# Two attentions and a feed-forward in one kernel: the next batch's values and both sets of transposes take other places in TensorE's row

## The chip, the cores and the metric

The kernel runs on one core of one Trainium2 chip. The metric is the device time of one execution in microseconds (us). The time before is the median of three runs, 399.38 us (396.07 to 399.92).

## The reference, cut to what matters

```python
# x, ctx: (16, 128, 128); 16 heads of 64
def self_attention(x):                    # over the 128 positions of a batch
    Q, K, V = x @ W_Q + b_Q, x @ W_K + b_K, x @ W_V + b_V
    P = softmax(Q @ K.T / 8)
    return (P @ V) @ W_O + b_O

def cross_attention(x1, ctx):             # per position, over the HEADS, not the positions
    q, k, v = x1 @ Wq.T + bq, ctx @ Wk.T + bk, ctx @ Wv.T + bv
    P2 = softmax(einsum('bshd,bsgd->bshg', q, k) / 8)
    out = einsum('bshg,bsgd->bshd', P2, v)          # then transposed and reshaped
    return out @ Wo.T + bo

x1 = layernorm(x  + self_attention(x))
x2 = layernorm(x1 + cross_attention(x1, ctx))
x3 = layernorm(x2 + feed_forward(x2))     # rms norm, up, gelu, down
```

## The kernel before, in words

The 16 batches go through a pipeline that is written out by hand as 16 calls of `step(s, ...)` on each engine (steps 3 to 14 are a loop of three rounds of four), followed by a tail that is written out instruction by instruction. Nothing is scheduled by a tool: each engine runs its own list in order, and semaphores with counts join the lists. In step s TensorE (PE) works on three batches at once. Part a is the scores and softmax of batch s, part bc the self-attention output and the cross-attention scores of batch s-1, part d the cross-attention output of batch s-2. Each group of four batches shares the projections of queries and keys, so a step also has a phase, s modulo 4: in phase 3, 0 and 1 there is group work (blocks A to D of `project_qk`, then E and F of `project_k2`) in the row, in phase 2 none.

PE's row in one step before the change, by the helpers' names:

- `transpose_p(s-1, 1)`: the second half of the transposes of the softmax result P of batch s-1, 8 heads, to PSUM banks 1 and 6. It waits for `p_ready`, which GpSimd (POOL) gives after `over_sum`. ScalarE (ACT) copies each bank to `pt` (`transposed`).
- blocks of `project_qk` or `project_k2`, in phases 0 and 1.
- `values(phase)`: the values of batch s, six products, to banks 7 and 0. They are 128x128 by 128x512 products of operands split in a high and a low part. ACT copies them out (`values_out`).
- `weighted(s)`: P transposed times the values, batch s-1. VectorE (DVE) copies the two halves out (`attention_out`, semaphore `ot_ready`).
- `scores(0)`: half of the scores of batch s, to banks 7 and 0. DVE takes their maxima (`score_max`), ACT the exponentials.
- `project_o`: the output projection of the self-attention, batch s-1. It waits for `ot_ready`, both halves.
- `transpose_p2`, then `scores(1)`, then `values2(0)` and `values2(1)` (the context's values, banks 2 and 3, copied out by DVE's `values2_out`, semaphore `v2s_ready`).
- the transpose of x1 (bank 7) and `transpose_x2` (bank 0), which ACT copies out.
- `weighted_v2`, `project_q2` (banks 2 and 3), `transpose_p(s, 0)` (the first half for batch s), in phase 3 block A, `project_o2` (the second output projection), `scores2`, and in phases 3 and 0 the first two units of the next block.

After `scores2` DVE runs `pick_own` (four operations) and `max2`. POOL then subtracts the maximum (`minus_max2`), ACT takes the exponential (`exp2`) and DVE the sums (`sums2`). In phases 2 and 3 DVE's list has this order at the start of a step:

```python
for u in range(2):
    attention_out(s, u)
    if d and not projecting:
        (sums2, inverse_sums2)[u](s)
```

So `sums2` stands between the two `attention_out` there. In phases 0 and 1 it stands earlier, beside the group work.

DVE's list goes on with `score_max(0)`, `score_max(1)`, `x2_out`, `stats1`, `block_diagonal` twice, `x1_out`, `inverse_sums(0)`, `score_max(2)`, `values2_out(0)`, `score_max(3)`, `values2_out(1)`, `regrouped`, `q2_out` twice, in phase 0 `c_low`, `inverse_sums(1)`, `stats2`, `pick_own`, `max2`. SyncE (SP) issues 16 DMAs per step, which spread the context values for `weighted_v2`.

Of the kernel before, what the change touches and what calls it, by code (L numbers as in the profile page):

```python
# [50 lines left out]
def build(nc, x_nat, x_t, ctx_t, w_qk, w_v, w_o, b_qk, b_v, b_o,  # L51
# [10 lines left out]
    with ctx:  # L62
# [110 lines left out]
        X1T, X2T = 7, 0  # L173
# [298 lines left out]
        def _(act):  # L472
# [75 lines left out]
            def step(s, h, g, phase, a, bc, d):  # L548
                par, b_par = phase % 2, 1 - phase % 2

                def transposed(u):

                    act.wait_ge(mm_t, 4 * s + u + 1 if u < 2 else 4 * s - 4 + u + 1)
                    dst, src = pt_part(u)
                    nc.scalar.activation(dst, src, ACT.Copy).then_inc(pt_ready, 1)  # L555
# [10 lines left out]
                def values_out(s, par):  # L566
                    for u in range(2):
                        act.wait_ge(mm_v, 2 * s + u + 1)
                        nc.scalar.activation(v[par][:, u * BANK:(u + 1) * BANK], bank(V_BANK[u]), ACT.Copy).then_inc(v_ready, 1)
# [13 lines left out]
                if bc:  # L583
                    transposed(2)
                    transposed(3)
# [15 lines left out]
                if a and bc:  # L601
                    values_out(s, par)
# [10 lines left out]
                if not static or s > 2:  # L613
                    x2_transposed(s - 1, X2T)
                if a:
                    exponentials(2)
# [4 lines left out]
                if phase == 3 and not static:  # L621

                    act.wait_ge(mm_v, 2 * s + 2)
                    x_high(g + 1)
# [9 lines left out]
                if static and s == 0:  # L634
# [3 lines left out]
                    split_hi(8)  # L638
                if a:
# [7 lines left out]
            for u in (2, 3):  # L647
                act.wait_ge(mm_t, 4 * (B - 1) + u + 1)
                dst, src = pt_part(u)
                nc.scalar.activation(dst, src, ACT.Copy).then_inc(pt_ready, 1)  # L650
# [33 lines left out]
        def _(dve):  # L684
# [140 lines left out]
            def step(s, h, g, phase, a, bc, d):  # L825
# [62 lines left out]
                if static and s == 0:  # L888
# [14 lines left out]
                    return  # L903
                if a and not (static and s == 1):
# [9 lines left out]
                if phase == 3 and not static:  # L914
                    x_low(g + 1)
# [132 lines left out]
        def _(pe):  # L1048
# [135 lines left out]
            def values(phase):  # L1184
                own = slice(phase * T, (phase + 1) * T)
                for u in range(2):
                    cols = slice(u * BANK, (u + 1) * BANK)
                    nc.tensor.matmul(bank(V_BANK[u]), xg_lo[:, own], wv_hi[:, cols], start=True, stop=False)  # L1188
# [25 lines left out]
            def step(s, h, g, phase, a, bc, d):  # L1214
# [64 lines left out]
                if bc:  # L1279
                    transpose_p(s - 1, 1)  # L1280
# [13 lines left out]
                if a and bc:  # L1294

                    pe.wait_ge(pt_ready, 4 * s - 4 + 2)
                    values(phase)
# [7 lines left out]
                elif a:  # L1305
# [4 lines left out]
                    pe.wait_ge(v_ready, 2 * s + 2)  # L1310
# [18 lines left out]
                if bc:  # L1329
# [3 lines left out]
                    for u in range(2):  # L1333
# [3 lines left out]
                        values2(u, own)  # L1337
                    if static and s == 1:
                        pe.wait_ge(in_perm, 16)
                    if a:  # L1340

                        pe.wait_ge(exp_ready, 4 * s + 1)
                    pe.wait_ge(x1_ready, s)
                    nc.tensor.transpose(bank(X1T, T), x1[:], perm[:]).then_inc(mm_x1t, 1)
                    if late:
                        if a:

                            pe.wait_ge(exp_ready, 4 * s + 2)
# [13 lines left out]
                if bc:  # L1362
                    project_q2(s, 1)
                if static and s == 0:
# [7 lines left out]
                    values(0)  # L1372
                    project_k2(0, "F", lambda r: read_k2(r, "E"), units=(0, 1))
                    pe.wait_ge(in_ident, 16)

                    pe.wait_ge(v_ready, 2)
                if a:
                    if late:

                        pe.wait_ge(xnt_ready, s - 2)  # L1380
                    transpose_p(s, 0)
                if static and s == 0:

                    project_k2(0, "F", lambda r: read_k2(r, "E"), units=(2, 3))
# [6 lines left out]
                if d:  # L1391
# [3 lines left out]
                    project_o2(s)  # L1395
                if phase == 3 and not static:
# [21 lines left out]
            transpose_p(B - 1, 1)  # L1418
# [149 lines left out]
```

## Time and profile before

| | us |
|---|---|
| median of 3 runs | 399.38 |
| lowest, highest | 396.07, 399.92 |
| the profiled execution, whole | 397.88 |
| its span, first to last instruction | 396.1 |
| PE busy in the span | 386.1 |
| DVE busy | 285.3 |
| ACT busy | 239.7 |
| POOL busy | 147.7 |

The span is the part of the profiled execution that the trace covers. 1.8 us lie around it. An engine's busy time is the union of its instructions' times. One minus its share is the time that it stood waiting.

### The profile page before, as it was taken

What the parts mean: (1) busy time and instruction counts of PE and PEld (TensorE: products, weight loads), DVE (VectorE), ACT (ScalarE), POOL (GpSimd) and SP (SyncE); (2) the same over time, 40 slices, a digit from 0 to 9 for tenths busy, and PEclk for the clock granted to TensorE, in tenths of its full rate; (3) what the DMA queues carried; (4) which work ended last, traced back from release to release, by engine and by line L of the source; (5) the groups of instructions that cost most, each with busy time, mean ns of one, the idle gap of its engine ahead of it and who ended that gap; (6) DMA issues with size and microseconds to landing.
All of it is one profiled execution on the core that took longest, in us unless ns stands there. A gap on an engine that the chain in (4) does not pass through costs nothing.

```text
span 396.1 us, 16460 instructions
## 1 busy us (share of the span) xinstructions
PE 386.1 (97%) x6836; PEld 335.3 (85%) x6836; DVE 285.3 (72%) x660; ACT 239.7 (61%) x815; POOL 147.7 (37%) x224
## 2 busy tenths in 40 slices
PE   8999899999999999999999999999999999999995
PEld 8787788878888888878988888878988888888985
DVE  4677778776749688776848778667757878677555
ACT  5685585745567475745668466655667566556451
POOL 0642445421414454422414454323315455323214
PEclk9999999999999999999999999999999999999999
DMA  7910212310100213110101113100101111211001
GB/s 238 370 48 8 47 31 44 88 31 7 38 22 15 51 29 96 33 25 8 42 16 25 40 35 89 40 18 8 38 20 30 40 36 25 48 40 25 28 29 53
DMA packets 43760, 19.37 MB, mean 49 GB/s; under 512 B 36592, under 2 KB 41200, under 8 KB 43696
## 3 DMA queue, kind: packets, MB, share of 16 engines
q1 hardware_dynamic: 42880, 16.88, 16.5%
q0 software_dynamic: 528, 1.45, 1.0%
q8 instruction: 54, 0.88, 0.9%
q10 hardware_dynamic: 288, 0.07, 0.1%
q14 instruction: 10, 0.08, 0.1%
HBM read 8.95 MB, written 1.05 MB: 25 GB/s over the span
## 4 chain that ended last, share of the span: by engine, by line
PE 91%; SPq 3%; DVE 2%; issue 1%; ACT 1%; DMA 1%; POOL 1%; POOLq 0%; DVEq 0%
PE ps L1255 8%; PE ps L1200 8%; PE ps L1077 7%; PE ps L1168 7%; PE ps L1105 7%; PE ps L1180 7%; PE ps L1057 5%; PE ps L1157 5%; PE ps L1059 5%; PE ps L1058 5%; PE ps L1096 4%; PE ps L1210 4%; PE ps L1133 3%; SPq L323 3%; PE ps L1188 3%; PE ps L1194 2%
## 5 line engine op out<-in xcount | busy, mean ns | idle before, releaser
L562 ACT ACTIVATE p<-ps,neg_max 128x128 f32<-128x128 f32 x256 | 90.0, 382 | 38.9 <-DVE neg_max L832 38.7
L409 POOL TENSOR_TENSOR p<-p,row_inv 128x1024 f32<-128x1024 f32 x32 | 60.7, 1897 | 64.4 <-DVE row_inv L838 64.4
L555 ACT ACTIVATE pt<-ps 128x512 f32<-128x512 f32 x62 | 34.3, 619 | 47.1 <-PE ps L1157 46.9
L562 ACT ACTIVATION_READ_ACCUMULATOR p<-ps,neg_max 128x1 f32 x256 | 57.4, 224 | 0.0
L832 DVE TENSOR_REDUCE neg_max<-ps 128x4 f32<-128x512 f32 x64 | 41.7, 675 | 5.1 <-PE ps L1255 4.0
L778 DVE TENSOR_TENSOR ot<-ps,bv 128x512 f32<-128x512 f32 x32 | 22.0, 689 | 25.0 <-PE ps L1180 24.8
L1168 PE MATMUL ps<-x1t,wq 128*64 128x64 f32 x1024 | 34.4, 224 | 2.1 <-issue 1.7
L1255 PE MATMUL ps<-kt,qt 64*64 64x128 f32 x1024 | 35.2, 275 | 0.0
L1168 PEld LDWEIGHTS ps<-x1t,wq 128*64 128x64 f32 x1024 | 31.8, 138 | 3.8 <-issue 2.7
L1105 PE MATMUL ps<-wo,ot 128*128 128x128 f32 x256 | 32.3, 279 | 0.5 <-DVE qt L810 0.5
L1200 PE MATMUL ps<-wo,ot 128*128 128x128 f32 x256 | 32.7, 281 | 0.0
L1180 PEld LDWEIGHTS ps<-pt,v 128*64 128x64 f32 x512 | 27.6, 137 | 5.8 <-ACT pt L555 3.3
L1255 PEld LDWEIGHTS ps<-kt,qt 64*64 64x64 f32 x1024 | 27.6, 132 | 5.4 <-issue 5.3
L1200 PEld LDWEIGHTS ps<-wo,ot 128*128 128x128 f32 x256 | 29.9, 191 | 2.7 <-issue 2.6
L1180 PE MATMUL ps<-pt,v 128*64 128x128 f32 x512 | 31.5, 276 | 0.0
L1105 PEld LDWEIGHTS ps<-wo,ot 128*128 128x128 f32 x256 | 30.0, 192 | 1.7 <-DVE qt L810 0.6
L1077 PE MATMUL ps<-cg,wk 128*64 128x128 f32 x512 | 29.9, 274 | 0.0
L402 POOL TENSOR_TENSOR rn<-ssm,minus_half 128x1 f32<-128x1 f32 x16 | 8.8, 549 | 56.3 <-DVE ssm L769 56.3
L1077 PEld LDWEIGHTS ps<-cg,wk 128*64 128x64 f32 x512 | 27.8, 137 | 1.0 <-issue 0.5
L1057 PE MATMUL ps<-xg_hi,wqk_hi 128*128 128x512 f32 x62 | 25.4, 409 | 0.4 <-issue 0.4
L1058 PE MATMUL ps<-xg_lo,wqk_hi 128*128 128x512 f32 x62 | 24.5, 395 | 0.0
L1059 PE MATMUL ps<-xg_hi,wqk_lo 128*128 128x512 f32 x62 | 24.5, 395 | 0.0
(158 smaller groups left out, 827.6 us busy)
## 6 DMA issues: line engine op xcount, KB each, us to landing
v<-v2s SPq DMA_DIRECT2D x256, 32.0 KB
xg<-x_t SPq DMA_DIRECT2D x4, 256.0 KB, 2.6
cg<-ctx_t SPq DMA_DIRECT2D x4, 256.0 KB, 2.7
wo<-w_o SPq DMA_DIRECT2D x2, 512.0 KB, 9.3
xres<-x_nat SPq DMA_DIRECT2D x15, 64.0 KB, 1.8
pt<-w_qk SPq DMA_DIRECT2D x3, 256.0 KB, 4.1
out<-x2b SPq DMA_DIRECT2D x3, 256.0 KB, 2.3
x2b<-w_v SPq DMA_DIRECT2D x1, 512.0 KB, 6.4
```

The source lines that it names most:

```text
L409: nc.gpsimd.tensor_tensor(ph, ph, row_inv[:, 8 * half:8 * half + 8].unsqueeze(2).to_broadcast([T, 8, T]), ALU.mult).then_inc(p_ready, 1)
L562: last = nc.scalar.activation(p[:, hd * T:(hd + 1) * T], bank(S_BANK[q])[:, pos * T:(pos + 1) * T], ACT.Exp, bias=neg_max[:, hd:hd + 1], a ...
L832: nc.vector.reduce_max(neg_max[:, first:first + 7:2], bank(S_BANK[q]).rearrange("p (h k) -> p h k", h=4), AX.X, negate=True).then_inc(max_ ...
L1057: nc.tensor.matmul(out_cols, w_hi_cols, m_hi, start=True, stop=False)
L1058: nc.tensor.matmul(out_cols, w_hi_cols, m_lo, start=False, stop=False)
L1059: return nc.tensor.matmul(out_cols, w_lo_cols, m_hi, start=False, stop=True)
L1077: last = nc.tensor.matmul(bank(BLOCK_BANKS[blk][r])[64 * ih:64 * ih + 64, i * 128:(i + 1) * 128], wk2[:, hd * DH:(hd + 1) * DH], own, star ...
L1105: last = nc.tensor.matmul(bank(O2, D), ot2[:, k * 128:(k + 1) * 128], wo2[:, k * D:(k + 1) * D], start=k == 0, stop=k == K - 1)
L1168: last = nc.tensor.matmul(bank(Q2[u])[64 * ih:64 * ih + 64, i * HALF:(i + 1) * HALF], wq2[:, hd * DH:(hd + 1) * DH], x1t[:, ih * HALF:(ih ...
L1180: last = nc.tensor.matmul(bank(PV_BANK[u])[64 * (i % 2):64 * (i % 2) + 64, (i // 2) * T:(i // 2 + 1) * T], v[b_par][:, hd * DH:(hd + 1) * ...
L1200: last = nc.tensor.matmul(bank(O, D), ot[:, c * T:(c + 1) * T], wo[:, c * D:(c + 1) * D], start=c == 0, stop=c == NC - 1)
L1255: mm = nc.tensor.matmul(bank(S_BANK[2 * half + i % 2])[qh * HALF:(qh + 1) * HALF, (i // 2) * T:(i // 2 + 1) * T], qt[rows, first:first + H ...
```

## The change

`values` leaves its place ahead of `weighted`. It now computes the values of the next batch, s+1, right behind `values2`, and waits for the exponentials that read banks 7 and 0. The x1 and x2 transposes stand behind it. They go to banks 2 and 3 instead of 7 and 0, and so wait until DVE has copied the context values out of these banks (`v2s_ready`). Both halves of the transposes of P of batch s stand together behind `project_o2` (in phase 3 the first half stays ahead of block A), ahead of `scores2`. None is left at the start of a step. ACT's list follows: `exponentials(2)`, then the two copies of the next values, then the copy of x1 transposed, and all four copies of P transposed at the end of a step. DVE's list changes in one place: in phase 3 `x_low` (the low part of the next group's x) stands ahead of `score_max(2)`, since the next values need it in this step.

```diff
-        X1T, X2T = 7, 0
+        X1T, X2T = 2, 3
...
 # ScalarE
-                if bc:
-                    transposed(2)
-                    transposed(3)
...
-                if a and bc:
-                    values_out(s, par)
...
-                if bc:
+                if phase == 3 and not static:
+
+                    act.wait_ge(mm_v, 2 * s + 2)
+                    x_high(g + 1)
+                if bc:
+                    exponentials(2)
+                    if not (static and s == B - 1):
+                        values_out(s + 1, b_par)
                     act.wait_ge(mm_x1t, s)
                     nc.scalar.activation(x1t[:], bank(X1T, T), ACT.Copy).then_inc(x1t_ready, 1)
...
                 if a:
                     transposed(0)
                     transposed(1)
                 if phase == 3 and not static:
                     qk_out(g + 1, "A")
+                if a:
+                    transposed(2)
+                    transposed(3)
...
 # VectorE
+                if phase == 3 and not static:
+                    x_low(g + 1)
                 if a and not (static and s == 1):
                     score_max(2)
...
 # TensorE
-                if bc:
-                    transpose_p(s - 1, 1)
...
-                if a and bc:
-
-                    pe.wait_ge(pt_ready, 4 * s - 4 + 2)
-                    values(phase)
                 if bc:
                     weighted(s, b_par)
...
-                    pe.wait_ge(v_ready, 2 * s + 2)
                     scores(0)
...
                         values2(u, own)
+                    if s < B - 1:
+                        if phase == 3:
+                            pe.wait_ge(x_lo, g + 2)
+
+                        values((phase + 1) % GB, lambda u: pe.wait_ge(exp_ready, 4 * s + u + 1))
...
-                    if a:
-
-                        pe.wait_ge(exp_ready, 4 * s + 1)
+
+                    pe.wait_ge(v2s_ready, 2 * s - 1)
                     pe.wait_ge(x1_ready, s)
                     nc.tensor.transpose(bank(X1T, T), x1[:], perm[:]).then_inc(mm_x1t, 1)
                     if late:
-                        if a:
-
-                            pe.wait_ge(exp_ready, 4 * s + 2)
+
+                        pe.wait_ge(v2s_ready, 2 * s)
                         transpose_x2(s - 1, X2T)
...
                     project_o2(s)
+                if a:
+                    if phase < 3 or static:
+
+                        if s < B - 1:
+                            pe.wait_ge(v_ready, 2 * s + 4)
+                        transpose_p(s, 0)
+                    transpose_p(s, 1)
```

The first place is PE's row from the second output projection of a step of phase 1 to the output projection of the next step, of phase 2. `L1105` is `project_o2`, `L1157` `transpose_p`, `L1210` `scores2`, `L1188` to `L1190` `values`, `L1180` `weighted`, `L1255` `scores`, `L1200` `project_o`. Before:

```order
L1157 MATMUL ps<-ident,p 128x64 [waits p_ready,xnt_ready]
L1105 MATMUL ps<-wo,ot 128x128 [waits ot2_by_dve,ot2_by_act,q2_ready]
L1210 MATMUL ps<-kb,qt 64x64 [waits k2_by_act,k2_by_dve,q2_ready]
L1157 MATMUL ps<-ident,p 128x64 [waits p_ready]
L1188 MATMUL ps<-wv_hi,xg_lo 128x512 [waits pt_ready]
...
L1180 MATMUL ps<-pt,v 64x128 [waits v_ready,pt_ready]
...
L1255 MATMUL ps<-kt,qt 64x128 [waits v_ready]
...
L1200 MATMUL ps<-wo,ot 128x128 [waits ot_ready,s2_ready]
```

After, in the changed kernel's line numbers (each two or three lower):

```order
L1102 MATMUL ps<-wo,ot 128x128 [waits ot2_by_dve,ot2_by_act,q2_ready]
...
L1154 MATMUL ps<-ident,p 128x64 [waits p_ready,v_ready]
...
L1154 MATMUL ps<-ident,p 128x64 [waits p_ready]
...
L1208 MATMUL ps<-kb,qt 64x64 [waits k2_by_act,k2_by_dve,q2_ready]
...
L1177 MATMUL ps<-pt,v 64x128 [waits v_ready,pt_ready]
...
L1253 MATMUL ps<-kt,qt 64x128 x16
L1198 MATMUL ps<-wo,ot 128x128 [waits ot_ready,s2_ready]
```

Between `scores2` and `project_o` stand only `weighted` and `scores(0)` now. The second half of the transposes and `values` have left this stretch.

The second place is PE's row from the context's values to `weighted_v2` (`L1096`) in a late step. `L1194` to `L1196` are `values2`, `L1344` is the transpose of x1, `L1112` that of x2. Before:

```order
L1194 MATMUL ps<-wv_hi,cg_lo 128x512 [waits c_lo,k2_by_dve]
...
L1196 MATMUL ps<-wv_lo,cg_hi 128x512
L1344 MATMUL ps<-perm,x 128x128 [waits x1_ready,exp_ready]
L1112 MATMUL ps<-ident,xn 128x128 [waits xn_ready,exp_ready]
L1096 MATMUL ps<-pt,v 64x64 [waits pb_ready,sum1_ready,v2_moved]
```

After:

```order
L1192 MATMUL ps<-wv_hi,cg_lo 128x512 [waits c_lo,k2_by_dve]
...
L1194 MATMUL ps<-wv_lo,cg_hi 128x512
L1186 MATMUL ps<-wv_hi,xg_lo 128x512 [waits exp_ready]
...
L1186 MATMUL ps<-wv_hi,xg_lo 128x512 [waits exp_ready]
...
L1339 MATMUL ps<-perm,x 128x128 [waits x1_ready,v2s_ready]
L1109 MATMUL ps<-ident,xn 128x128 [waits xn_ready,v2s_ready]
L1093 MATMUL ps<-pt,v 64x64 [waits pb_ready,sum1_ready,v2_moved]
```

The six products of the next values (`L1186` to `L1188`) have come in, and the two transposes wait for `v2s_ready` in place of `exp_ready`.

## Rows read from the trace of the kernel before

**Rows 1.** The page, part 1: busy time, share of the span, instructions.

```profile
PE 386.1 (97%) x6836; PEld 335.3 (85%) x6836; DVE 285.3 (72%) x660; ACT 239.7 (61%) x815; POOL 147.7 (37%) x224
```

**Rows 2.** The page, part 4: the chain that ended last, shares by engine.

```profile
PE 91%; SPq 3%; DVE 2%; issue 1%; ACT 1%; DMA 1%; POOL 1%; POOLq 0%; DVEq 0%
```

**Rows 3.** Windows: stretch, its length, busy us of each engine, clock, DMA.

```profile
31.00:47.00 16.00, 14.59 (x302) 12.45 (x300) 11.12 (x24) 9.68 (x40) 5.72 (x7) 1.00 0.12 26
117.00:134.00 17.00, 17.00 (x370) 14.74 (x366) 13.16 (x31) 10.48 (x43) 6.62 (x9) 1.00 0.11 27
```

**Rows 4.** Timeline of PE, step 9 (phase 1) into step 10: start, us, line.

```profile
206.94 2.05 PE L1200 MATMUL ps<-wo,ot 128*128 128x128 f32 x16
...
211.67 0.27 PE L1344 MATMUL ps<-perm,x 128*128 128x128 f32 x1
...
215.96 0.71 PE L1157 MATMUL ps<-ident,p 64*128 64x64 f32 x16
216.60 2.05 PE L1105 MATMUL ps<-wo,ot 128*128 128x128 f32 x16
...
219.67 0.71 PE L1157 MATMUL ps<-ident,p 64*128 64x64 f32 x16
221.89 1.97 PE L1180 MATMUL ps<-pt,v 128*64 128x128 f32 x32
...
224.82 2.05 PE L1200 MATMUL ps<-wo,ot 128*128 128x128 f32 x16
```

**Rows 5.** Timeline of DVE, the same stretch.

```profile
211.40 0.64 DVE L832 TENSOR_REDUCE neg_max<-ps 128x4 f32<-128x512 f32 x1
...
213.15 0.68 DVE L788 TENSOR_TENSOR v2s<-ps,bv_row 128x512 f32<-128x512 f32 x1
...
216.06 0.69 DVE L810 TENSOR_TENSOR qt<-ps,bq 128x512 f32<-128x512 f32 x1 [0.69 <-PE ps L1168]
216.67 0.19 DVE L838 RECIPROCAL row_inv<-row_sum 128x8 f32<-128x8 f32 x1
...
219.81 0.48 DVE L818 TENSOR_SCALAR s<-ps,own_j 128x256 f32<-128x256 f32 x1 [0.22 <-PE ps L1210]
...
221.88 0.42 DVE L728 TENSOR_REDUCE mx<-s 128x16 f32<-128x256 f32 x1
...
223.64 0.41 DVE L732 TENSOR_REDUCE sum<-s 128x16 f32<-128x256 f32 x1
223.97 0.68 DVE L778 TENSOR_TENSOR ot<-ps,bv 128x512 f32<-128x512 f32 x1
```

**Rows 6.** Timeline of POOL, the same stretch.

```profile
216.94 1.90 POOL L409 TENSOR_TENSOR p<-p,row_inv 128x1024 f32<-128x1024 f32 x1 [3.07 <-DVE row_inv L838]
...
222.38 0.62 POOL L373 TENSOR_TENSOR s<-s,mx 128x256 f32<-128x256 f32 x1 [1.90 <-DVE mx L728]
```

**Rows 7.** Timeline of ACT, the same stretch.

```profile
203.69 1.16 ACT L569 ACTIVATE v<-ps 128x512 f32<-128x512 f32 x2
...
210.52 0.44 ACT L523 ACTIVATE xn<-x,rn 128x128 f32<-128x128 f32 x1
...
212.36 0.37 ACT L562 ACTIVATE p<-ps,neg_max 128x128 f32<-128x128 f32 x1
...
213.74 1.13 ACT L519 ACTIVATE ot<-ps 128x512 f32<-128x512 f32 x1
...
223.04 0.42 ACT L514 ACTIVATE s<-s 128x256 f32<-128x256 f32 x1 [0.44 <-POOL s L373]
```

**Rows 8.** Timeline of ACT and of DVE, step 11 (phase 3).

```profile
248.97 0.65 ACT L484 ACTIVATE xg_hi<-xg 128x512 fp32r<-128x512 f32 x1
...
249.65 0.69 DVE L695 TENSOR_TENSOR xg_lo<-xg,xg_hi 128x512 fp32r<-128x512 f32 x1 [0.56 <-ACT xg_hi L484]
```

**Rows 9.** The chain in order of time: start, us, line; two products of `values`.

```profile
202.49 0.43 PE ps L1188
...
203.39 0.23 PE ps L1188
```

More of the change, by code:

```diff
@@ L551, in transposed @@
                 def transposed(u):
[L553 removed]
+                    act.wait_ge(mm_t, 4 * s + u + 1)
                     dst, src = pt_part(u)
@@ L609, in step @@
                     normed_x2(s - 1)
+                if phase == 3 and not static:
+                    act.wait_ge(mm_v, 2 * s + 2)
+                    x_high(g + 1)
                 if bc:
+                    exponentials(2)
+                    if not (static and s == B - 1):
+                        values_out(s + 1, b_par)
                     act.wait_ge(mm_x1t, s)
                     nc.scalar.activation(x1t[:], bank(X1T, T), ACT.Copy).then_inc(x1t_ready, 1)
-                if not static or s > 2:
+                elif a:
+                    exponentials(2)
+                if s_late(s):
                     x2_transposed(s - 1, X2T)
-                if a:
-                    exponentials(2)
                 if phase == 0 and bc and a:
@@ L620, in step @@
                     c_high(g)
-                if phase == 3 and not static:
-                    act.wait_ge(mm_v, 2 * s + 2)
-                    x_high(g + 1)
                 if static and s == B - 1:
@@ L638, in step @@
                     split_hi(8)
+                    values_out(1, 1)
                 if a:
@@ L643, in step @@
                     qk_out(g + 1, "A")
+                if a:
+                    transposed(2)
+                    transposed(3)
             run_steps(act, step)
[L647 to L650, printed above, removed]
             exp2(B)
@@ L913, in step @@
                     values2_out(s, 1, d)
-                if phase == 3 and not static:
-                    x_low(g + 1)
                 if static and s == B - 1:
@@ L1182, in weighted, with values @@
                     last.then_inc(mm_pv, 1)
-            def values(phase):
+            def values(phase, before):
                 own = slice(phase * T, (phase + 1) * T)
@@ L1187, in values @@
                     cols = slice(u * BANK, (u + 1) * BANK)
+                    before(u)
                     nc.tensor.matmul(bank(V_BANK[u]), xg_lo[:, own], wv_hi[:, cols], start=True, stop=False)
@@ L1362, in step @@
                 if bc:
+                    if late:
+                        pe.wait_ge(xnt_ready, s - 2)
                     project_q2(s, 1)
@@ L1371, in step @@
                     pe.wait_ge(w_lo, WV_SPLIT)
-                    values(0)
-                    project_k2(0, "F", lambda r: read_k2(r, "E"), units=(0, 1))
+                    values(0, lambda u: None)
+                    project_k2(0, "F", lambda r: read_k2(r, "E"))
+                    values(1, lambda u: pe.wait_ge(v_ready, u + 1))
                     pe.wait_ge(in_ident, 16)
[L1376 to L1380, printed above, removed]
+                if phase == 3 and not static:
+                    pe.wait_ge(v_ready, 2 * s + 4)
                     transpose_p(s, 0)
-                if static and s == 0:
-                    project_k2(0, "F", lambda r: read_k2(r, "E"), units=(2, 3))
                 if phase == 3 and not static:
@@ L1416, in _ @@
                 step(s, s // 2, s // GB, s % GB, s < B, 1 <= s <= B, s >= 2)
-            transpose_p(B - 1, 1)
             pe.wait_ge(wup_split, 2)
```

6 lines of the change are left out of this document (3 added, 3 removed).

## Prediction

> **What bounds the kernel now.** I read the page's busy times first, then the chain that ended last, then windows over single steps, then the timelines of one step engine by engine. PE is busy for 386.1 of 396.1 us [rows 1], and the chain is PE for 91% [rows 2]. A window of one step shows no idle time on PE at all, 17.00 of 17.00 us, with the granted clock at 1.00 [rows 3]. The change removes no product: the same matmuls run in another order. So there are at most the 10 us that PE idles to be gained. The question is the other one: PE has no waits now because each result that it needs is ready just before. Where the new order asks for one earlier, the difference appears in full. So I laid the new order of each engine over the rows of one step, with the rows' durations, and looked for the operand that comes last.
>
> I count from M, the start of `project_o` (206.94 in step 9), and from E, the end of `scores2` (219.67, where the next row starts) [rows 4]. Durations below are distances between starts, since neighbouring instructions overlap.
>
> **First term: project_o waits for DVE, steps of phases 2 and 3.** After E came `transpose_p` and `values`, 221.89-219.67 = 2.22 us, then `weighted` and `scores(0)`, 224.82-221.89 = 2.93 us [rows 4]. Now only the 2.93 us lie between E and `project_o`. What DVE must do in this time has not moved. `pick_own` starts 0.14 after E and `max2` at 2.21 [rows 5]. It runs 0.33 to the next start, so DVE is free at E+2.54. The first `attention_out` takes 0.61 to the next start, as `q2_out` of the same size does (216.06 to 216.67) [rows 5]. Behind it stands `sums2`, which needs the exponential. POOL's subtraction starts at E+2.71 and takes 0.62, and ACT's exponential 0.42 from E+3.37 to E+3.79 [rows 6, 7]. ACT is free by then: its four copies end near E+0.4. `sums2` runs from E+3.83 for 0.33 (223.64 to 223.97), the second `attention_out` from E+4.16 for 0.68, and `project_o` can start at E+4.89. The wait is 4.89-2.93 = 1.96 us. It hits the entries of steps 2, 3, 6, 7, 10, 11, 14 and 15. The first of them is counted with the start below, so 7 x 1.96 = 13.7 us. In phases 0 and 1 ten units of `project_qk` (each half of `values`, some 0.75 us) or six of `project_k2` (each half of `weighted`, 0.95 us) lie between E and `weighted` and still cover DVE's part.
>
> **Second term: the x2 transpose waits for values2_out.** From M on DVE works without a gap, and it ends `values2_out(1)` at 213.15+0.68 = M+6.89, released at M+6.93 or so; PE can go at M+6.97 [rows 5]. PE comes to the x1 transpose at M+4.73 now [rows 4]. With six products of 0.233 us in front (1.40) this is M+6.13, and the x2 transpose would start at M+6.24. It waits 0.73 us. The exponentials that `values` itself waits for end at 210.52 = M+3.58 [rows 7], before PE asks, and cost nothing. In steps 4, 5, 6, 8, 9, 10, 12, 13, 14 that is 9 x 0.73 = 6.6 us. Behind it ACT's new order would bite next: `score_max(2)` ends at M+5.10, four exponentials take 213.74-212.36 = 1.38, two copies of values 1.16, the copy of x1 0.28, so x1 transposed is ready at M+8.0, and PE asks for it behind `weighted_v2`, which has as many products as `scores2` (1.09 us), at M+8.17. That is a margin of 0.2 us, so I put it at nothing; had it no cover it would be worth its lateness in each step. Step 2, without an x2 transpose, waits for it by 0.5.
>
> In phase 3 `x_low` stands ahead of `score_max(2)`. `x_high` takes 0.65 us on ACT [rows 8] and can start at M+4.01, after the copy at 210.52 (0.44 long) [rows 7]. `x_low` runs from M+4.72 and takes 0.60 of DVE's time. DVE would have been at `score_max(2)` at M+4.46 [rows 5], so all behind it comes 0.86 later, and the x2 transpose at M+7.8 instead of 6.24: 1.56 us, 3 x 1.56 = 4.7 us. Step 15 has no next values in front. Its x2 transpose comes up at M+4.84 and waits until M+6.97: 2.1 us, of which 0.85 us replace waits that this step has already. I take 1.3.
>
> **Third term: the second half of the transposes waits for POOL.** `q2_out(1)`, the reciprocal and `over_sum` are a chain: from the end of `project_q2` (215.96 in the rows) to the end of `over_sum` at 216.94+1.90 = 218.84 [rows 4 to 6] plus its release it is 2.94 us. PE needs this half after `project_o2` (216.60 to 219.67 is 3.07 us and holds it and `scores2`; as many products as `project_o`, 2.05 less an overlap of 0.07, it takes 1.98, which leaves 1.09 for `scores2`) and the first half (215.96 to 216.60, 0.64), 2.62 us later: a wait of 0.32 us in steps 2, 5, 6, 9, 10, 13, 14, 15, 2.6 us. In phase 0 `c_low`, of the size of `x_low`, stands before the reciprocal, 0.61 more: 0.93 x 3 = 2.8 us. In phase 3 block A covers it.
>
> **Fourth term: the moved half was a cover.** Units 2 of blocks B and E wait for `pick_own`, which is through at E+2.1. Before, two units and a set of transposes (0.64) stood between. Now only the units: six products like `values` for block B (2.22-0.64 = 1.58), a wait of 0.5, and 32 like `weighted` for block E (1.97 less the overlap), 0.2. Three of each make 2.1 us.
>
> **Start.** In step 0 both halves stand together ahead of `weighted`: it waits until ACT has made three copies after the first half, 3 x 0.55, against 0.64 of PE work, 1.05 us. The first half waits for the last copy of `values`, some 0.65. I take 1.7 us. Step 1 to 2 has the 1.96 of the first term and a third term over 1 us, but it idles already: PE is busy 14.59 of 16 us from 31 to 47 [rows 3], and these 1.4 us are swallowed. I take 1.9 us.
>
> **What the order gives back.** The first product of this kind behind another kind takes 0.43 instead of 0.23 us on the chain [rows 9]. `values` behind `values2` pays that no more in 11 batches, and block B, no longer split, in 3: 14 x 0.2 = 2.8 us gained.
>
> **What is neutral.** SP's 16 DMAs now wait for `weighted_v2` (M+8.2) instead of `values2_out` (M+6.9). They have a whole, longer step to land before the next `weighted_v2`, so nothing. The tail has the same rows in the same order but for the moved half, whose 0.64 us a wait for x1 takes up. Banks 7 and 0 are free when `scores(0)` comes.
>
> **The sum.** 13.7 + 6.6 + 0.5 + 4.7 + 1.3 + 2.6 + 2.8 + 2.1 + 1.7 + 1.9 - 2.8 = 35.1 us. The profiled execution took 397.9 us, its span 396.1. So 433.0 us. That execution is 1.5 us under the median of 399.4. Steps stay whole: each term is counted from an M or an E on which both engines meet, so they add and do not overlap. I forecast 433.
>
> A rule is weighed here. The rows show a granted clock of 1.00 in both windows, also in the one with 1.4 us of idle PE [rows 3]. The Trainium skill, "TensorE: Matmul & The Clock Gate", section "A second HAM failure mode: psum-queue depth-cycling", says that a PE which idles briefly between groups of matmuls, again and again, can drop back to the low clock. By the rows the new waits of up to 2 us cost only themselves and the sum is 433; by the rule it would be the third rival below. The trace of before speaks for the rows, though its waits are shorter and rarer.
>
> **Rivals.** *The waits are hidden (the other side).* If DVE delivered `attention_out(1)` within 2.93 us of E and `values2_out(1)` by M+6.2, only the gain of 2.8 us would stay: 395.1 us. The mechanism is the cheaper change between kinds of product [rows 9], at `values2` to `values`, and it decides once the waits are under 0.1 us a step, 15 steps. Against it: DVE needs 2.40 + 0.60 + 0.68 = 3.7 us from E by its own work alone, without POOL and ACT. Chance 0.03.
>
> *Half the first term.* If `sums2` finds its operand earlier than I chain it, the second `attention_out` ends at E+2.54+0.60+0.33+0.68 = 4.15 at best, and the wait is 1.25 instead of 1.96 us; with the second term absorbed by half as well, 7 x 0.7 + 3.3 + 2.4 = 10.6 less: 422 us. For it speaks that sub-chains of three engines are long in my sum, against it that POOL's and ACT's starts are read, not assumed. Chance 0.14.
>
> *The clock falls.* No row has the low level of 1.2 GHz. At half the clock a stretch takes twice as long, an estimate. If `project_o`, which stands right behind each of the 8 long waits, ran so, that is 8 x 2.05 = 16 us more: 449 us. Chance 0.05.
>
> *ACT's copies bite.* If the margin of 0.2 us at x1 transposed is not there, ACT adds 0.3 to 0.5 us in 13 steps, 4 to 6 us: 438 us. Chance 0.14. The forecast itself has 0.64.
>
> **How the numbers follow.** The range from 421 to 441 takes in the forecast with some 4 us either way for the rounding of fifteen small waits, the half term and the copies, and leaves out 0.08. The runs of before spread over 1%, about what a measurement of this kernel can tell from no change. Only the first rival is not slower by over 1%: it gives 0.7% faster, so same 0.03, and I keep 0.01 for faster by more. Slower by over 1%: 0.96.
>
> **What the profile after would show.** PE's busy share falls from 97% to near 90%, with about 2 us idle before `project_o` in steps of phases 2 and 3, released by DVE's `ot`, and about 0.7 us before the x2 transpose, released by DVE's `v2s`, 1.5 in phase 3. `transpose_p` shows short waits for POOL's `p`. The chain has less PE and more DVE, POOL and ACT. Each round of four steps is about 9 us longer. If `project_o` does not wait, the first term is wrong and with it the forecast. If PE's clock is under 1.00 in a window, the third rival holds. If the copy of x1 transposed releases `project_q2`, ACT's order is what I undervalued.

## The result

The changed kernel takes 438.0 us (median of four runs, 436.28 to 439.31) against 398.2 us before, a ratio of 1.101 with a 95% interval of 1.097 to 1.105. The forecast was 433, with a range of 421 to 441. The profiled execution took 439.3 us, its span is 437.5.

The page of the changed kernel, parts 1 and 4: busy times and the chain that ended last, shares by engine.

```profile
PE 396.1 (91%) x6836; PEld 343.3 (78%) x6836; DVE 287.7 (66%) x660; ACT 240.9 (55%) x815; POOL 149.2 (34%) x224
...
PE 65%; DVE 20%; issue 6%; POOL 5%; ACT 2%; SPq 1%; DVEq 0%; POOLq 0%; DMA 0%
```

The same 6836 matmuls keep PE busy for 10.0 us more than before [rows 1], and PE idles 437.5 - 396.1 = 41.4 us instead of 10.0. The chain was PE for 91% [rows 2]; now DVE, POOL and ACT hold 27% of it. The span itself is longer by 41.4 us too (396.1 before, the same figure by chance). Of these, 31.4 us are new idle time of PE and 10.0 us are longer busy time. Most of the 10.0 goes with the clock, of which more below: in the first experiment, whose profiled execution has no fall of the clock, PE is busy for 388.4 us. The waits by what PE waited for (us in total, times, longest):

```profile
PE ps L1198 <- DVE ot L775: 16.2, 8, 2.3
PE ps L1109 <- DVE v2s L785: 6.7, 11, 0.9
PE ps L1154 <- POOL p L409: 5.7, 11, 1.4
PE ps L1054 <- DVE s L819: 1.7, 3, 0.6
...
PE ps L1177 <- ACT pt L554: 1.1, 1, 1.1
...
PE ps L1339 <- DVE v2s L785: 0.8, 1, 0.8
PE ps L1074 <- DVE s L819: 0.8, 3, 0.3
```

These are the prediction's terms one by one: `project_o` (L1198) on `attention_out`, the x2 transpose (L1109) on `values2_out`, the second half of the transposes (L1154) on `over_sum`, blocks B and E (L1054, L1074) on `pick_own`. The 1.1 us of `weighted` (L1177) belong to the start. The timeline of PE for step 9 into step 10, the stretch of [rows 4], shows them in place:

```profile
231.42 2.05 PE L1198 MATMUL ps<-wo,ot 128*128 128x128 f32 x16
...
238.37 0.33 PE L1109 MATMUL ps<-ident,xn 128*128 128x128 f32 x1 [0.58 <-DVE v2s L785]
...
244.68 0.71 PE L1154 MATMUL ps<-ident,p 64*128 64x64 f32 x16 [0.26 <-POOL p L409]
...
246.42 1.97 PE L1177 MATMUL ps<-pt,v 128*64 128x128 f32 x32
248.31 1.10 PE L1253 MATMUL ps<-kt,qt 64*64 64x128 f32 x32
251.40 2.81 PE L1198 MATMUL ps<-wo,ot 128*128 128x128 f32 x16 [1.98 <-DVE ot L775]
254.00 0.63 PE L1081 MATMUL ps<-ident,p 128*128 128x128 f32 x2
254.57 1.70 PE L1253 MATMUL ps<-kt,qt 64*64 64x128 f32 x32
```

M is 231.42, E is 246.42 and the next M 251.40. The x2 transpose starts at M+6.95 (forecast M+6.97), the next `project_o` at E+4.98 (forecast 4.89). The chain in order of time shows the path across the three other engines from E on:

```profile
248.63 0.43 DVE mx L725
249.06 0.07 issue
249.13 0.63 POOL s L373
...
249.79 0.42 ACT s L514
...
250.24 0.42 DVE sum L729
250.66 0.61 DVE ot L775
251.26 0.14 issue
251.40 0.68 PE ps L1198 x4
```

DVE's `attention_out` of the second half (250.66) starts only when `sums2` (250.24) is through, which has waited for POOL and ACT.

What I gave a chance of its own stands in the last three rows of the timeline: `project_o` takes 2.81 us behind the wait instead of 2.05, and `scores(1)` 1.70 instead of 1.10. Windows over this place (stretch, length, busy us by engine, granted clock, DMA):

```profile
231.42:246.42 15.00, 14.17 (x309) 12.37 (x305) 9.90 (x24) 10.34 (x42) 6.63 (x9) 1.00 0.12 26
246.42:251.40 4.98, 3.00 (x70) 2.61 (x65) 4.12 (x10) 0.52 (x2) 0.62 (x1) 1.00 0.22 46
251.40:255.40 4.00, 4.00 (x34) 3.67 (x38) 2.88 (x11) 3.19 (x17) 2.18 (x5) 0.63 0.03 6
```

Behind the 1.98 us in which PE stood, the granted clock has a mean of 0.63 in four us. Windows of 1 us over the whole span show five such falls, in steps 1, 6, 7, 10 and 11, each with 1 us windows at 0.50, the low level of 1.2 GHz. The kernel before had none in its profiled execution. Four of the falls stand behind the wait of `project_o`. The fall of step 1 stands behind two other waits, 0.73 and 1.13 us, and `weighted`, which takes 1.97 us in the kernel before, takes 3.35 there:

```profile
33.60 3.35 PE L1177 MATMUL ps<-pt,v 128*64 128x128 f32 x32 [1.13 <-ACT pt L554]
```

### The profile page after: what moved, and what is told of

Read it like the earlier page. It is cut to its first block, busy times and chain, and to the rows that moved or that the text cites. A ratio compares the mean times of both kernels' runs of the same rounds, so it can differ in the third digit from the quotient of the medians.

```text
span 437.5 us, 16468 instructions
## 1 busy us (share of the span) xinstructions
PE 396.1 (91%) x6836; PEld 343.3 (78%) x6836; DVE 287.7 (66%) x660; ACT 240.9 (55%) x815; POOL 149.2 (34%) x224
## 4 chain that ended last, share of the span: by engine, by line
PE 65%; DVE 20%; issue 6%; POOL 5%; ACT 2%; SPq 1%; DVEq 0%; POOLq 0%; DMA 0%
PE ps L1198 8%; PE ps L1165 7%; PE ps L1074 5%; PE ps L1253 5%; PE ps L1054 4%; PE ps L1055 4%; PE ps L1056 4%; PE ps L1102 4%; PE ps L1093 4%; DVE s L819 4%; POOL p L409 3%; DVE v2s L785 3%; PE ps L1177 3%; PE ps L1208 3%; DVE neg_max L829 3%
## 5 line engine op out<-in xcount | busy, mean ns | idle before, releaser
L561 ACT ACTIVATION_READ_ACCUMULATOR p<-ps,neg_max 128x1 f32 x256 | 55.2, 216 | 0.0
L1198 PE MATMUL ps<-wo,ot 128*128 128x128 f32 x256 | 36.4, 301 | 16.2 <-DVE ot L775 16.2
L1198 PEld LDWEIGHTS ps<-wo,ot 128*128 128x128 f32 x256 | 33.2, 209 | 19.4 <-issue 19.4
L1253 PE MATMUL ps<-kt,qt 64*64 64x128 f32 x1024 | 37.1, 286 | 0.0
L1253 PEld LDWEIGHTS ps<-kt,qt 64*64 64x64 f32 x1024 | 29.4, 140 | 6.3 <-issue 6.1
L1165 PEld LDWEIGHTS ps<-x1t,wq 128*64 128x64 f32 x1024 | 31.4, 138 | 3.1 <-issue 1.7
L1177 PE MATMUL ps<-pt,v 128*64 128x128 f32 x512 | 32.7, 283 | 1.1 <-ACT pt L554 1.1
L1102 PE MATMUL ps<-wo,ot 128*128 128x128 f32 x256 | 32.3, 279 | 0.0
L807 DVE TENSOR_TENSOR qt<-ps,bq 128x512 f32<-128x512 f32 x32 | 22.1, 692 | 14.6 <-PE ps L1165 14.5
L1177 PEld LDWEIGHTS ps<-pt,v 128*64 128x64 f32 x512 | 29.0, 141 | 3.3 <-issue 1.5
L1102 PEld LDWEIGHTS ps<-wo,ot 128*128 128x128 f32 x256 | 30.0, 192 | 1.2 <-DVE qt L807 0.2
L1074 PE MATMUL ps<-cg,wk 128*64 128x128 f32 x512 | 29.7, 274 | 0.8 <-DVE s L819 0.8
L373 POOL TENSOR_TENSOR s<-s,mx 128x256 f32<-128x256 f32 x16 | 10.1, 633 | 59.3 <-DVE mx L725 59.3
L1074 PEld LDWEIGHTS ps<-cg,wk 128*64 128x64 f32 x512 | 27.8, 137 | 2.3 <-DVE s L819 1.5
L1154 PE MATMUL ps<-ident,p 64*128 64x64 f32 x512 | 22.6, 228 | 6.6 <-POOL p L409 5.7
L721 DVE COPY ot<-ps 128x512 f32<-128x512 f32 x16 | 18.0, 1125 | 15.3 <-PE ps L1093 15.3
```

The costliest lines, as they stand in the source:

```text
L561: last = nc.scalar.activation(p[:, hd * T:(hd + 1) * T], bank(S_BANK[q])[:, pos * T:(pos + 1) * T], ACT.Exp, bias=neg_max[:, hd:hd + 1], a ...
L807: nc.vector.tensor_tensor(qt2[:].rearrange("p (t h) -> p t h", h=H)[:, :, heads], bank(Q2[u]).rearrange("p (h t) -> p t h", h=8), bq2[:, h ...
L1074: last = nc.tensor.matmul(bank(BLOCK_BANKS[blk][r])[64 * ih:64 * ih + 64, i * 128:(i + 1) * 128], wk2[:, hd * DH:(hd + 1) * DH], own, star ...
L1102: last = nc.tensor.matmul(bank(O2, D), ot2[:, k * 128:(k + 1) * 128], wo2[:, k * D:(k + 1) * D], start=k == 0, stop=k == K - 1)
L1154: mm = nc.tensor.transpose(bank(T_BANK[2 * half + e])[:, i * HALF:(i + 1) * HALF], p[rows, hd * T:(hd + 1) * T], ident[rows, rows])
L1165: last = nc.tensor.matmul(bank(Q2[u])[64 * ih:64 * ih + 64, i * HALF:(i + 1) * HALF], wq2[:, hd * DH:(hd + 1) * DH], x1t[:, ih * HALF:(ih ...
```

## The experiments

The kernels were run in three sets, each next to the kernel before, which had medians of 397.3 to 397.8 us there. Clocks below are those of the profiled execution unless others are named.

**The first term: what project_o waits for.** One edit in DVE's list of the changed kernel:

```diff
                     for u in range(2):
                         attention_out(s, u)
-                        if d and not projecting:
-                            (sums2, inverse_sums2)[u](s)
+                    if d and not projecting:
+                        sums2(s)
+                        inverse_sums2(s)
```

> The changed kernel with one edit in VectorE's list: in phases 2 and 3 sums2 and inverse_sums2 stand behind both attention_out instead of between them. Theory (project_o waits for the second attention_out, which waits for sums2 and so for POOL and ACT): the wait of 1.96 us falls to about 0.9, 7 or 8 times 1.1 = 8.6 us less, and the granted clock no longer falls behind the waits of steps 6, 7, 10 and 11, some 5 us more: 424 us. Rival (any wait there drops the clock, however short): 429 us. Rival (the wait is for pick_own alone, sums2 is beside the point): 438 us, unchanged.

Measured: 430.2 us, ratio to the kernel before 1.083 (1.078 to 1.088). PE's timeline in this run, from step 6 to the start of step 7:

```profile
148.66 2.02 PE L1199 MATMUL ps<-wo,ot 128*128 128x128 f32 x16 [0.98 <-DVE ot L775]
155.90 0.33 PE L1110 MATMUL ps<-ident,xn 128*128 128x128 f32 x1 [0.86 <-DVE v2s L785]
...
168.17 2.02 PE L1199 MATMUL ps<-wo,ot 128*128 128x128 f32 x16 [1.22 <-DVE ot L775]
```

The wait falls from 1.98 to 0.98 us in the first of these steps and to 1.22 in the second, and no 1 us window of the profiled execution is under 1.00 in clock. So the serial path over POOL and ACT was about half of the wait. The rival that `pick_own` alone was to blame falls. The rival that any wait drops the clock had the nearer number, 429 us, but not the mechanism: the waits of `project_o` of 0.98 to 1.93 us did not drop it here. The other three executions have mean clocks of 0.991 to 0.996, so a fall or two in them is likely (the run below with one fall has 0.996).

The size was 6 us short of what I expected, and the second row says why: the x2 transpose now starts at 155.90-148.66 = M+7.24 instead of M+6.95. DVE's sums did not vanish, they stand behind M now, where DVE bounds PE again. In phase 3 they delay `x_low`: the next values wait 2.1 us for it in three steps by PE's list, against 0.9 us in the run filled with 8 products below, and the step from 168.17 to 199.27 takes 31.10 us, where the filled run takes 30.46.

**The clock.** Products of a zero tile fill the wait, in the changed kernel. They go into the bank which `project_o` then overwrites, so the output stays the same:

```diff
                     ring_wait(2)
+                    if phase >= 2:
+                        for _ in range(12):
+                            nc.tensor.matmul(bank(O, D), warm[:], warm[:], start=True, stop=True)
                     pe.wait_ge(ot_ready, 2 * s)
```

> The changed kernel with 12 additional 128x128x128 products of the zero tile warm ahead of project_o in phases 2 and 3, into project_o's bank, which project_o then overwrites: about 1.5 us of extra PE work inside the wait of 1.96 us, so that PE stands idle for 0.5 us only. Theory (part of the loss is the clock, which falls behind the long wait): the wait for VectorE ends at the same point, the clock stays at 1.00 in steps 6, 7, 10 and 11, and the time falls by 4 falls of up to 1.7 us, less what the slower products hide in the next wait: 432 to 434 us. Rival (the fallen clock costs nothing, since PE waits anyway): 438 us.

Measured: 440.6 us, ratio 1.108 (1.104 to 1.113). The clock stayed at 1.00, but the 12 products took longer than the wait that they were to fill:

```profile
148.88 2.94 PE L1310 MATMUL ps<-warm 128*128 128x128 f32 x24
151.67 1.95 PE L1198 MATMUL ps<-wo,ot 128*128 128x128 f32 x16
```

From 148.88 to 151.67 they hold PE for 2.79 us, 0.8 more than the wait, in 8 steps. The run does not give the price of the clock. It was made again with 8.

> As the first run with filling products, but 8 instead of 12, since 12 took 2.79 us and were longer than the wait itself. 8 take 1.86 us, less than the 1.96 us of the wait. Theory (the fallen clock costs time of its own): project_o starts where it did, the clock stays at 1.00 in steps 6, 7, 10 and 11, and each of these four steps is 0.9 to 1.6 us shorter: 433 to 434 us. Rival (the clock's fall is paid by time that PE would wait anyway): 438 us.

Measured: 434.2 us, ratio 1.093 (1.088 to 1.097). Its timeline at step 10:

```profile
245.59 2.05 PE L1310 MATMUL ps<-warm 128*128 128x128 f32 x16
247.55 2.05 PE L1198 MATMUL ps<-wo,ot 128*128 128x128 f32 x16
249.44 0.38 PE L1081 MATMUL ps<-ident,p 128*128 128x128 f32 x2
249.75 1.10 PE L1253 MATMUL ps<-kt,qt 64*64 64x128 f32 x32
```

`project_o` still starts 4.89 us after E (242.66), but it takes 2.05 and `scores(1)` 1.10 us. PE does more work and the kernel is 3.8 us faster by the medians, about 1 us for each of the four falls avoided; the fifth, in step 1, is still there. All four executions have a mean clock of 0.996 to 0.999, against 0.980 to 0.984 in the changed kernel, and each is faster than each of the changed kernel's. The two intervals of the ratio just touch (1.088 to 1.097 against 1.097 to 1.105), so the sign is well supported and the size is not to be taken to the tenth. In the two traces the four stretches from one `project_o` to the next that hold a fall in the changed kernel are 1.7 us (step 6 to 7), 1.4 (7 to 8), 1.0 (10 to 11) and 1.2 us (11 to 12) shorter in the filled run, 5.2 us together.

**The banks alone.** The kernel before, with values and all transposes of P where they were:

```diff
-        X1T, X2T = 7, 0
+        X1T, X2T = 2, 3
...
-                        pe.wait_ge(exp_ready, 4 * s + 1)
+                    pe.wait_ge(v2s_ready, 2 * s - 1)
                     pe.wait_ge(x1_ready, s)
...
-                            pe.wait_ge(exp_ready, 4 * s + 2)
+                        pe.wait_ge(v2s_ready, 2 * s)
                         transpose_x2(s - 1, X2T)
...
+                    if late:
+                        pe.wait_ge(xnt_ready, s - 2)
                     project_q2(s, 1)
...
```

The last place goes with the banks: `project_q2` writes bank 3 next, so now it waits for ACT's copy of x2 transposed, and no longer the first transposes of P. PE's list shows no wait for this copy.

> The kernel before with the banks of the x1 and x2 transposes alone changed to 2 and 3, with their waits for v2s_ready; values and the transposes of P stay where they were. Theory (VectorE is busy without a gap from M to M+6.9, and delivers values2_out(1) only then): the x2 transpose waits until M+6.97 instead of M+4.84 in 13 steps, 27.7 us, and the x1 transpose 1.0 us in steps 1 and 2: about 427 us. Rival (VectorE would take values2_out earlier if asked, the banks are free): 398 us.

Measured: 435.4 us, ratio 1.093 (1.089 to 1.098). PE in step 5:

```profile
126.72 2.05 PE L1200 MATMUL ps<-wo,ot 128*128 128x128 f32 x16
...
132.47 0.33 PE L1342 MATMUL ps<-perm,x 128*128 128x128 f32 x1 [0.87 <-DVE v2s L788]
133.67 0.33 PE L1112 MATMUL ps<-ident,xn 128*128 128x128 f32 x1 [0.87 <-DVE v2s L788]
133.93 1.98 PE L1096 MATMUL ps<-pt,v 64*64 64x64 f32 x64
```

The x2 transpose starts at M+6.95 here too: DVE's list sets this time whatever PE does. That is 2.1 us late in each step, as expected. The kernel is 8 us slower than that. In windows of 1 us the clock falls to 0.50 behind these two short waits in 8 of the 13 steps that have both, and `weighted_v2` takes 1.98 us there instead of the 1.16 that it takes in the filled run below. That run filled the two waits with 3 products each:

```diff
+                    pe.wait_ge(sum1_ready, s)
+                    for _ in range(3):
+                        nc.tensor.matmul(bank(O, D), warm[:], warm[:], start=True, stop=True)
                     pe.wait_ge(v2s_ready, 2 * s - 1)
...
+                        for _ in range(3):
+                            nc.tensor.matmul(bank(O, D), warm[:], warm[:], start=True, stop=True)
                         pe.wait_ge(v2s_ready, 2 * s)
```

> The kernel with the banks alone changed, with 3 products of the zero tile ahead of the wait of the x1 transpose and 3 ahead of that of the x2 transpose (into project_o's bank, after its sum has been taken), some 0.70 us each inside waits of 0.87 us. Theory: the 8 falls of the clock disappear, 1.5 us each where PE has no later wait to absorb them, so 435.4 - 10 to 13 = 422 to 426 us. Rival (the clock's fall is absorbed, the waits alone make the loss): 435 us.

Measured: 426.1 us, ratio 1.072 (1.068 to 1.076), 9.3 us less than without the filling.

```profile
132.92 0.33 PE L1345 MATMUL ps<-perm,x 128*128 128x128 f32 x1 [0.19 <-DVE v2s L788]
133.08 0.83 PE L1348 MATMUL ps<-warm 128*128 128x128 f32 x6
134.12 0.33 PE L1112 MATMUL ps<-ident,xn 128*128 128x128 f32 x1 [0.20 <-DVE v2s L788]
134.37 1.16 PE L1096 MATMUL ps<-pt,v 64*64 64x64 f32 x64
```

M is 127.17 in this run, so the x2 transpose starts at M+6.95 as before, and the clock stays at 1.00 in all 13 steps. The bank change alone costs some 28 us in waits and 9 us in clock. In the changed kernel `values` lies over two thirds of the same wait, which is why the banks cost far less there than alone. The move of values without the new banks was not run.

**The transposes alone.** The kernel before with both halves behind `project_o2`; they are gone from their old places, and ACT's copies follow:

```diff
...
                     project_o2(s)
+                if a:
+                    if phase < 3 or static:
+                        if late:
+                            pe.wait_ge(xnt_ready, s - 2)
+                        transpose_p(s, 0)
+                    transpose_p(s, 1)
...
```

> The kernel before with the two halves of the transposes of P moved behind project_o2 as in the change, values and banks as before. Theory: values still covers 1.58 us ahead of project_o, so it waits 0.4 us 8 times (3), the second half waits for POOL 0.3 us in 8 steps and 0.9 in 3 (5.4), units 2 of blocks B and E wait (2.1), the start costs 1, block B gives back 0.6: about +11, 409 us. No fall of the clock. Rival (the moved transposes make nearly all of the loss): above 425 us.

Measured: 414.1 us, ratio 1.041 (1.037 to 1.045), 5 us above what I expected. The rival, above 425 us, falls. The waits on PE (total, times, longest):

```profile
PE ps L1153 <- POOL p L409: 6.1, 10, 2.2
PE ps L1101 <- DVE qt L806: 3.0, 6, 1.5
PE ps L1196 <- DVE ot L774: 2.8, 7, 0.4
PE ps L1053 <- DVE s L818: 1.7, 3, 0.6
```

Three of the four are as worked out (5.4, 3 and, with block E, 2.1 expected). I had missed the second: with no transposes between `project_q2` and `project_o2`, the latter comes 0.64 us earlier and waits for DVE's `q2_out`. In the changed kernel that wait is not there; I take it that the wait of the x2 transpose gives DVE the time, which no run tests. This kernel also had one fall of the clock near 45 us, which I had not expected.

**The values alone.** The changed kernel with the second half of the transposes back at the start of the next step, on both engines:

```diff
...
+                if bc:
+                    transpose_p(s - 1, 1)
                 if phase == 0 and a and bc:
...
                         transpose_p(s, 0)
-                    transpose_p(s, 1)
...
```

> The changed kernel with the second half of the transposes of P put back at the start of the next step, on PE and on ACT; values, banks, x_low and the first half stay changed. Theory: 0.64 us more cover ahead of project_o, which waits 1.3 instead of 1.96 us (8 x 0.64 = 5 less), no waits for POOL's p (5.4 less) and none of units 2 of blocks B and E (2.1 less), block B is split again (0.6 more), fewer falls of the clock (3 less): 438 - 15 = 423 us. Rival (the moved transposes cost next to nothing, values is the whole loss): above 433 us.

Measured: 420.6 us, ratio 1.057 (1.052 to 1.062).

```profile
PE ps L1114 <- DVE v2s L790: 7.9, 13, 0.9
PE ps L1182 <- ACT pt L554: 6.6, 9, 1.1
PE ps L1203 <- DVE ot L780: 4.8, 8, 0.7
```

The total is near what I expected, and the parts are not. `weighted` (L1182) now follows the transposes directly and waits for ACT to copy them, 6.6 us; `project_o` waits that much less, since both waits lie between the same two points. The moved half of the transposes costs 438.0 - 420.6 = 17 us of the change, the clock included: this run has two falls, near 34 and 359 us, in place of five.

**ACT's copies as the next wait.** The changed kernel with DVE's second context copy ahead of the last maxima:

```diff
-                if a:
-                    score_max(3)
                 if bc:
                     values2_out(s, 1, d)
+                if a:
+                    score_max(3)
```

> The changed kernel with one edit: values2_out(1) ahead of score_max(3) on VectorE. Theory: the x2 transpose waits 0.6 us less, but PE then asks for x1 transposed at M+7.6 and ACT has it at M+8.0 behind the next values' copies, so 0.4 of the 0.6 come back as a wait of project_q2 on ACT; 12 times 0.2 us: 435 to 436 us. Rival (ACT has it in time): 12 times 0.6 us less, 431 us.

Measured: 431.2 us (429.3 to 434.4), ratio 1.082 (1.078 to 1.085). The rival was right. PE waits 0.3 us once for the x2 transpose, where it waited 6.7 us in 11 steps. What came in its place is small. In step 5 `project_q2` starts at 139.35, 1.23 us behind `weighted_v2` (138.12) where it is 1.10 in the changed kernel, just when ACT has ended its copy of x1 transposed (138.99 + 0.31 = 139.30):

```profile
139.35 2.08 PE L1165 MATMUL ps<-x1t,wq 128*64 128x64 f32 x64
...
138.99 0.31 ACT L613 ACTIVATE x1t<-ps 128x128 f32<-128x128 f32 x1
```

So 0.1 us came back and not 0.4. With M at 131.51 the copy was through at M+7.8; my M+8.0 was 0.2 us too late. In the changed kernel's own trace ACT starts this copy at 238.89, which is M+7.47, and ends it at M+7.8 too. The profiled execution has five falls of the clock, as many as the changed kernel's.

**Three edits of order together**, and the same on the kernel that moves values only. The edits are the two above and, on ACT, the copies of x1 and x2 transposed ahead of the next values' copies.

> The changed kernel with three edits of order: sums2 behind both attention_out on VectorE, values2_out(1) ahead of score_max(3) on VectorE, and on ACT the copies of x1 and x2 transposed ahead of the next values' copies. Theory: from the first edit 430 us as measured, and the second with the third take 0.6 us from the x2 transpose's wait in 12 steps, 7 us: 423 us. Rival (VectorE's later score_max(3) delays ACT's last exponentials and POOL, which takes it back at the second half of the transposes): 428 to 430 us.

Measured: 424.3 us, ratio 1.065 (1.059 to 1.071), near the 423 of the theory. Not all of its parts held: PE's wait for `x_low` grew to 3.9 us in three steps, 2.6 us in one of them, and the profiled execution has three falls of the clock, near 34, 51 and 82 us.

> The kernel that moves values and banks but not the second half of the transposes, with the three edits of order (sums2 behind both attention_out, values2_out(1) ahead of score_max(3), copies of x1 and x2 transposed ahead of the next values' copies). Theory: of 22 us that the move of values costs, project_o's wait falls from 1.3 to 0.3 us in 8 steps (8 less) and the x2 transpose's by 0.6 in 12 (7 less), and no fall of the clock is left (2 less): 405 us. Rival (in the last run x_low's wait in phase 3 grew to 2.6 us once and ACT's later copies of values hold up the transposes): 410 us or more.

Measured: 411.5 us (406.8 to 413.3), ratio 1.030 (1.023 to 1.036). The rival had the number and half of the cause: PE's waits for `x_low` make 3.5 us in three steps. The longest of PE's waits in this run:

```profile
PE ps L1184 <- ACT pt L554: 6.6, 9, 1.1
```

`project_o` hardly waits any more (0.2 us once), but `weighted` still waits for ACT's copies by some 0.7 us in each of 8 steps, which the wait of `project_o` had hidden from my sum. It is the best version with the values moved, and still 3% behind the kernel before.

**A version that could beat both.** Only the gain from fewer changes of kind of product was left, and one move in the kernel before takes part of it:

```diff
                 if phase == 3 and not static:
+                    transpose_p(s, 1)
                     project_qk(g + 1, "B", lambda r: pe.wait_ge(sum2x_ready, s - 1) if r == 0 else read(1, (g + 1, "A")),
```

> The kernel before with one move: at the end of a step of phase 3 the second half of the transposes of P stands ahead of units 0 and 1 of block B instead of between units 1 and 2. Theory: block B is no longer split, which saves one change of kind of product (0.2 us) in three steps, unit 2 still finds pick_own through (0.64 + 1.58 us behind the end of scores2, needed at 2.1): 0.6 us less than before, 397.5 us, not to be told from no change by the times, but visible in the trace as 0.2 us less from the end of scores2 to the next project_o. Rival (the transposes there wait for POOL, or unit 2 for pick_own): up to 1 us more.

Measured over five rounds: 397.6 against 397.3 us, ratio 1.001 (0.999 to 1.003), no difference. The trace does not show the 0.2 us either: from the end of `scores2` at 256.74 to the next `project_o` at 270.49 it is 13.75 us, and 13.75 us in the kernel before (257.06 to 270.81). The row of block B's unit 2 shows a cost that I had not counted:

```profile
258.98 0.50 PE L1057 MATMUL ps<-xg_hi,wqk_hi 128*128 128x512 f32 x1
```

It starts 0.33 us behind the product before it and the next one 0.33 us behind it, as behind a change of kind, though nothing of another kind stands between. It comes at E+2.24, and by the prediction's rows `pick_own` is through at E+2.1; whether it waited for this, no run tells. I found no version that beats the kernel before.

## Why the prediction was right

**The method held.** From step 6 to step 7 the kernel before took 17.03 us from one `project_o` to the next, without idle time (136.87 to 153.90). The terms for an entry into phase 2 (0.73, 0.32 and 1.96, less 0.2) make it 19.84. The changed kernel has 19.98 from step 9 to 10 (231.42 to 251.40). For the step of phase 0 it was 24.32 (182.62 to 206.94), and 0.73, 0.93 and 0.2 less 0.2 make 25.98. The changed kernel has 26.00 (205.42 to 231.42). The filled run, in which only one fall of the clock is left, has a span of 431.7 us, and the sum without the clock gives 396.1 + 35.1 = 431.2.

That the two agree to 0.5 us is in part luck. The sum adds each wait to a span that already held 10 us of idle time, and some of it was swallowed: from step 9 to 10 the kernel before took 17.88 us, 0.60 of them idle, so that this step grew by 2.1 and not by 2.8. From the first `project_o` to the last, the filled run is 31.8 us longer than the kernel before, where the terms make 33.4. The start went the other way. I gave it 1.7 us; the first `project_o` comes 4.5 us later in the changed kernel (38.14 against 33.68) and 3.9 us in the filled run (37.57), of which the fall of the clock in step 1 makes about 1.5.

**First term**, 13.7 us in seven steps: 13.9, and 2.3 more in step 2, which was counted with the start, so 16.2 in eight. Right, with the cause shown by the edit of DVE's order. **Second term**, about 13 us: PE's list shows 6.7 + 0.8. Part of the difference is how idle time is counted (the transpose starts 0.73 us late in step 9, 0.58 is called idle), part is real: in steps with a fallen clock PE comes later to the transpose and waits less. With the clock kept up it is 7.8 us. The phase 3 part was too large by 0.2 us a step. In the filled run's step 7, where M is 171.20, the transpose starts at M+7.57 and not M+7.8:

```profile
175.66 0.67 DVE L692 TENSOR_TENSOR xg_lo<-xg,xg_hi 128x512 fp32r<-128x512 f32 x1
...
178.77 0.33 PE L1109 MATMUL ps<-ident,xn 128*128 128x128 f32 x1 [0.64 <-DVE v2s L785]
```

`x_low` starts at M+4.46, as soon as DVE comes to it, and not at M+4.72. **Third term**, 5.4 us: 5.7 in PE's list, but 1.4 of this is a wait in step 1, which the sum had as swallowed. In the steps that the term names it is 4.3: 0.26 us where I had 0.32, and 0.85 in phase 0 where I had 0.93; in step 15 PE's list has none. **Fourth**, 2.1: 1.7 + 0.8. **ACT's copies** do not bite in these steps (one wait of 0.4 us in step 2, where I had 0.5), and the margin was larger than I put it.

**Where it was off** is the rule that I weighed and set aside. The rows before, I wrote, speak for waits that cost only themselves. They did not here: the clock fell five times, and the total came 5 us above the forecast. This term stands at nothing in the sum; the filled run puts it at 3.8 us for four falls. The Trainium skill ("TensorE: Matmul & The Clock Gate", section "A second HAM failure mode: psum-queue depth-cycling") names frequent short idle times between groups of matmuls as a cause. The trace agrees: the five falls stand behind waits of 1.13 to 2.02 us. The 1.4 us of scattered idle time in one window of the kernel before was no test of it. As a rival I gave it 0.05 and 16 us. It came in part, as an addition to the forecast and not in its place, about 1 us for each fall. The range held it because of its upper margin, which was meant for other things, and not because of this rival. That is luck.

**What stays open.** Why the clock fell in steps 6, 7, 10 and 11 and not in 2, 3, 14 and 15, whose waits are as long (1.98 to 2.26 us), no run tells. In the run with `values2_out(1)` moved it fell in steps 3, 6, 7, 11 and 15 under the same waits of `project_o`, so the place is not fixed by the wait alone.

## What to carry to other kernels

When one engine is full, count the work between the instruction that starts a side chain and the one that needs its result, and take every product out of this stretch as a wait of its own length until the chain is shown to be shorter; here 2.2 us of matmuls moved away became a wait of 1.98 us. A buffer that is free "in time" is free when the copying engine's list gets to it, so lay the new reader against that list, not against the data's own readiness. If an engine must wait often, price the clock with the wait: filling the wait with idle products gave back 4 us in one kernel and 9 in another.

## What the runs showed of the hardware

The granted clock fell to 0.50 behind two waits of 0.87 us, 1.2 us apart, in 8 of 13 steps, and behind single waits of 1.98 and 2.02 us in 4 of 8. It did not fall in the profiled execution of the first experiment, whose waits of `project_o` are 0.98 to 1.93 us, nor in that of the kernel before, with idle gaps up to 0.74 us in its 15 steps. Products of zeros kept it up: 8 of them in a wait of 1.98 us, or 3 in each of two waits of 0.87. A plain 128x128x128 product of 32-bit floats is two records in the trace and holds PE for 2.79/12 = 0.23 us.
